# All gathers of a chunk wait for both rounds of the products of the step ahead

## The chip, the cores and the metric

The kernel runs on one core of one Trainium2 chip. A core has five engines that work side by side, each with its own queue of instructions: TensorE (PE; its weight loads are listed apart as PEld), VectorE (DVE), ScalarE (ACT), GpSimd (POOL) and SyncE (SP). They wait for each other through semaphores only. The metric is device time in microseconds (us): 590.68 is the median of 3 runs of the kernel before (590.22 to 592.27).

## The reference

It is a recommendation tower for 2048 samples in float32. Cut to what matters here:

```python
e = stack([tbl_f[ids[:, f]] for f in range(26)])      # 2048 x 26 x 64, rows of 26 tables
x = layer_norm(dense @ Wd.T, gd, bd)                   # 2048 x 128
y = layer_norm(e @ Ws.T, gs, bs)                       # 2048 x 26 x 128
y = layer_norm(einsum('bne,pn->bep', y, Wsi), gsi, bsi)
T = concatenate([x[:, None], swapaxes(y, 1, 2)])       # 2048 x 33 x 128
Z = einsum('bnd,bmd->bnm', T, T)                       # the products: 33 x 33 per sample
z = layer_norm(Z[lower triangle] @ Wl.T, gl, bl)       # first 384 columns are kept
h = relu(relu([z, dense] @ W_top1 + b1) @ W_top2 + b2)
out = h @ W_top3
```

The 53248 table rows of 64 values (2048 x 26) have to be fetched by index. That is the gather.

## The kernel before, in words

The samples are split into 16 units of 128. A unit is worked in 4 chunks; chunk c of unit u has the number k = 4u+c here. Its 1664 rows of the tables lie in `emb[:, u % 3]` as 13 tiles of 128 partitions with two rows side by side. One indirect DMA on GpSimd's queue, L314, fetches 128 rows (one half of a tile), so there are 26 of them in a unit, in four groups for c = 0 to 3: 8, 6, 6 and 6 (`HALVES`, which also splits each group in a first part of 4 gathers and a second of 4, 2, 2 and 2). `emb` has three buffers (`EB`).

The order of work is written out by hand as a pipeline of steps s: each engine runs through the same steps, and in a step it does fixed parts of chunks of different age. On TensorE step s holds, in this order:

- `turn` of chunk s-1 (L382): transposes of the gathered tiles into `bank_t`. It waits for all gathers of its chunk to land (`emb_in`). It raises `turned`.
- `mix` of chunk s-2 (L405): the mixing of the 26 rows into `bank_u`. It raises `mixed`.
- `gram` of chunk s-1 (L391), and `project` of chunk s-2 (L416).
- `products` of chunk s-4 (L430), in two rounds of 16 matmuls: round 0 into `bank_z`, round 1 into `bank_t`, which raise `z_done` by one each (`NR` = 2).
- then, in some steps only, matmuls of the later layers: `top1` (L465), `flat` (L442), `top2`, `dense_x`, `turn_z` and others.

ScalarE copies what comes out of the banks, VectorE scales and sums. The copies of the products go to `zbig`, from which SyncE's queue moves them once per unit.

GpSimd's queue holds nothing but the gathers, in the order of the chunks. Ahead of the gathers of chunk k it waits for `mixed` (the buffer of `emb` is free) and for `turned` of chunk k-2. These two waits stand in L306 and L307. Ahead of the second part of a group it waits in L310 for `z_done` at 2(k-5)+1, which is round 0 of the products of chunk k-5. TensorE does those products in step k-1; the transposes of chunk k stand in step k+1. `after` leaves a wait out while its value is zero or less, so L310 waits from chunk 5 on (at chunk 5 for round 0 of chunk 0).

Only GpSimd's block is changed. `turn`, `products` and the last lines of the diff are enough to follow it.

Of the kernel before, what the change touches and what calls it, by code (L numbers as in the profile page):

```python
# [63 lines left out]
HALVES = ((0, 2), (2, 4)), ((4, 6), (6, 7)), ((7, 9), (9, 10)), ((10, 12), (12, 13))  # L64
# [3 lines left out]
NR = len(ROUNDS)  # L68
# [106 lines left out]
def dlrm(nc, x_in, out):  # L175
    with ExitStack() as ctx:
        def sb(name, shape, dt=F32):
            return ctx.enter_context(nc.sbuf_tensor(name, shape, dt))
# [4 lines left out]
        def sem(name):  # L183
            return ctx.enter_context(nc.semaphore(name))
# [50 lines left out]
        part = sb("part", [P, MAXD])  # L235
# [32 lines left out]
        xcol_ok, z_done, zc_ok, sumcol_ok = sem("xcol_ok"), sem("z_done"), sem("zc_ok"), sem("sumcol_ok")  # L268
# [15 lines left out]
        def after(eng, s, value):  # L284

            if value > 0:
                eng.wait_ge(s, value)
# [12 lines left out]
        @block.gpsimd  # L300
        def _(pool):
            pool.wait_ge(ids_ok, 1)
            for u in range(NU):
                e = u % EB
                for c in range(4):
                    after(pool, mixed, 4 * (u - EB) + min(c + 2, 4))  # L306
                    after(pool, turned, 4 * u + c - 1)  # L307
                    for part, (t0, t1) in enumerate(HALVES[c]):
                        if part == 1:
                            after(pool, z_done, NR * (4 * u + c - 5) + 1)  # L310
                        for t in range(t0, t1):
                            for a in range(2):
                                col = 2 * TILES * u + 2 * t + a
                                pool.indirect_dma_start(  # L314
                                    emb[:, e, t, D * a:D * a + D], None, x_in["tables"],
                                    bass.IndirectOffsetOnAxis(ap=ids[:, col:col + 1], axis=0),
                                ).then_inc(emb_in[e][c], 16)
# [827 lines left out]
```

## Time and profile before

| | |
|---|---|
| median of 3 runs | 590.68 us |
| profiled execution: time | 590.11 us |
| its span, first to last instruction | 588.3 us |
| PE busy | 523.2 us (89%) |
| DVE busy | 431.7 us (73%) |
| ACT busy | 339.3 us (58%) |
| POOL busy | 394.8 us (67%) |
| gathers, L314 | 416, mean 949 ns, idle before them 130.3 us |
| first and last gather start | 4.3 and 524.4 us |
| gather, issue to landing | 2.4 us (median) |
| granted TensorE clock, mean | 0.983 |

How to read it: busy time is time in which an engine works on instructions, not time for which it is needed. "Idle before" is the time that the engine stood still just ahead of a group of instructions, with what ended it; "issue" means that the profile shows nothing that it waited for. For a gather the busy time ends when GpSimd has issued it; the data land later. A start time in the timeline is counted from the first instruction, and start plus duration is the end.

### The profile page before, as it was taken

How to read it: one execution, taken by the hardware profiler on the slowest of the kernel's cores; microseconds unless marked ns; L12 is line 12 of the kernel's file. 1: busy time of each engine (PE TensorE's matmuls, PEld its weight loads, DVE VectorE, ACT ScalarE, POOL GpSimd, SP SyncE). 2: the span in 40 equal slices, each digit the busy share in tenths (PEclk: the TensorE clock that was granted, in tenths of full speed). 3: DMA queues.
4: the chain of work that ended last, by engine and by line, in shares of the span. 5: the costliest groups of instructions: out<-in, count | busy, mean ns of one | idle time of the engine just before them, and what ended most of it. 6: DMA issues, size and time to landing. Idle time of an engine off the chain costs nothing.

```text
span 588.3 us, 11685 instructions
## 1 busy us (share of the span) xinstructions
PE 523.2 (89%) x4327; PEld 382.3 (65%) x4327; DVE 431.7 (73%) x806; ACT 339.3 (58%) x731; POOL 394.8 (67%) x420
## 2 busy tenths in 40 slices
PE   0557889597999999997999999998999999989888
PEld 0435656474778667776677767766777767856657
DVE  3579998689677977697877967796787977787210
ACT  1235666466657765575766765675657765766223
POOL 5777777777777777777777777777777777750000
PEclk9997999899899999999999999999999999999999
DMA  6911121212111121212121221212121211110100
GB/s 214 372 47 26 28 54 27 53 28 52 29 42 38 39 62 28 52 30 71 28 46 33 45 56 35 45 31 69 29 52 27 52 31 43 38 34 17 27 0 1
DMA packets 28152, 29.89 MB, mean 51 GB/s; under 512 B 9784, under 2 KB 20544, under 8 KB 27712
## 3 DMA queue, kind: packets, MB, share of 16 engines
q0 software_dynamic: 13312, 13.66, 12.2%
q1 hardware_dynamic: 14456, 15.29, 8.2%
q8 instruction: 35, 0.57, 0.4%
q10 hardware_dynamic: 328, 0.20, 0.1%
q14 instruction: 21, 0.17, 0.1%
HBM read 23.01 MB, written 0.01 MB: 39 GB/s over the span
## 4 chain that ended last, share of the span: by engine, by line
POOL 46%; PE 26%; issue 19%; DMA 4%; DVE 3%; ACT 1%; ACTq 1%; POOLq 0%; SPq 0%
POOL emb L314 46%; PE bank_h L442 5%; PE bank_u L405 4%; DMA emb<-in_tables,ids 3%; PE bank_m L465 3%; PE bank_y L416 3%; PE bank_g L391 2%; PE bank_z L430 2%; PE bank_t L382 2%; PE bank_t L430 1%; PE bank_m L526 1%; DVE part L910 1%; ACTq L774 1%; PE bank_g L490 1%; PE bank_m L533 0%
## 5 line engine op out<-in xcount | busy, mean ns | idle before, releaser
L314 POOL DMA_INDIRECT emb<-in_tables,ids x416 | 394.6, 949 | 130.3 <-issue 123.1
L662 ACT ACTIVATE sq<-tt 128x512 f32<-128x512 f32 x128 | 131.1, 1133 | 4.6 <-DVE tt L963 3.4
L932 DVE TENSOR_TENSOR prod<-bank_g,emb 128x512 f32<-128x512 f32 (+1 forms) x64 | 37.6, 588 | 89.0 <-PE bank_g L391 88.5
L442 PE MATMUL bank_h<-wz,zr 128*128 128x512 f32 x192 | 93.2, 610 | 3.1 <-ACT zt L727 2.1
L405 PE MATMUL bank_u<-mix_w,emb 128*128 128x192 f32 (+4 forms) x512 | 86.0, 314 | 9.7 <-DVE emb L951 9.7
L405 PEld LDWEIGHTS bank_u<-mix_w,emb 128*128 128x128 f32 x512 | 80.3, 200 | 10.9 <-DVE emb L951 10.9
L963 DVE TENSOR_TENSOR tt<-bank_y,biasc 128x512 f32<-128x512 f32 x128 | 81.9, 681 | 2.5 <-PE bank_y L416 2.5
L644 ACT COPY embt<-bank_t 128x512 f32<-128x512 f32 (+1 forms) x64 | 32.5, 507 | 82.4 <-PE bank_t L382 82.2
L980 DVE TENSOR_TENSOR tt<-tt,bank_z 128x1024 f32<-128x1024 f32 x64 | 78.1, 1220 | 2.2
L970 DVE TENSOR_REDUCE ssum<-sq 128x32 f32<-128x1024 f32 x64 | 77.5, 1211 | 1.1 <-ACT sq L662 1.0
L416 PE MATMUL bank_y<-us,proj 64*128 64x512 f32 x256 | 73.0, 647 | 0.7 <-ACT us L654 0.7
L430 PEld LDWEIGHTS bank_z<-tt 128*64 128x64 f32 x1024 | 35.4, 137 | 48.5 <-issue 47.4
L391 PE MATMUL bank_g<-gram_w,embt 128*128 128x128 f32 x416 | 61.9, 290 | 1.7 <-ACT embt L644 1.7
L382 PE MATMUL bank_t<-eye,emb 128*128 128x128 f32 x208 | 36.3, 290 | 27.5 <-DMA emb<-in_tables,ids 27.5
L654 ACT COPY us<-bank_u 128x512 f32<-128x512 f32 x64 | 37.5, 586 | 40.2 <-PE bank_u L405 40.1
L391 PEld LDWEIGHTS bank_g<-gram_w,embt 128*128 128x128 f32 x416 | 55.2, 202 | 2.7 <-ACT embt L644 2.5
L382 PEld LDWEIGHTS bank_t<-eye,emb 128*128 128x128 f32 x208 | 25.1, 146 | 48.5 <-DMA emb<-in_tables,ids 37.5
L442 PEld LDWEIGHTS bank_h<-wz,zr 128*128 128x128 f32 x192 | 33.8, 190 | 30.7 <-issue 26.8
L649 ACT ACTIVATE std<-var 128x8 f32<-128x8 f32 (+1 forms) x64 | 13.6, 212 | 56.4 <-DVE var L942 54.1
L430 PE MATMUL bank_z<-tt 128*64 128x68 f32 x1024 | 44.5, 229 | 0.0
L430 PE MATMUL bank_t<-tt 128*64 128x68 f32 x1024 | 41.2, 223 | 0.0
L465 PE MATMUL bank_m<-zt,w 128*128 128x256 f32 x168 | 40.8, 379 | 0.0
(121 smaller groups left out, 622.5 us busy)
## 6 DMA issues: line engine op xcount, KB each, us to landing
emb<-in_tables,ids POOLq DMA_INDIRECT x416, 2.4
zs<-zbig SPq DMA_DIRECT2D x62, 40.5 KB
zs<-zbig SPq DMA_DIRECT2D x62, 36.0 KB
dense<-in_dense SPq DMA_DIRECT2D x8, 256.0 KB, 5.1
wfull<-in_wfull SPq DMA_DIRECT2D x1, 2048.0 KB, 10.2
wz<-in_wrows SPq DMA_DIRECT2D x1, 1536.0 KB, 13.2
w<-in_w SPq DMA_DIRECT2D x1, 1280.0 KB, 13.9
zs<-zbig SPq DMA_DIRECT2D x62, 16.5 KB
```

What stands on the lines that cost most here:

```text
L314: pool.indirect_dma_start(emb[:, e, t, D * a:D * a + D], None, x_in["tables"], bass.IndirectOffsetOnAxis(ap=ids[:, col:col + 1], axis=0),) ...
L382: mm = pe.transpose(bank_t[:, P * (t - t0):P * (t - t0) + P], emb[:, e, t, :], eye[:, :])
L391: mm = pe.matmul(bank_g[:, o:o + P], embt[:, k % 2, o:o + P], gram_w[:, :], start=True, stop=True)
L405: mm = pe.matmul(bank_u[:, o:o + PR * cnt], emb[:, e, t, :], mix_w[:, t, :, :].rearrange("p s v -> p (s v)")[:, w0:w0 + PR * cnt], start=( ...
L416: mm = pe.matmul(bank_y[a][:, :], proj[q, :], us[q, h % 2, :], start=True, stop=True)
L430: mm = pe.matmul(o_bank[TILE * q:TILE * q + TILE, o:o + ZC * WIDE], some[:, C0 * WIDE:ZC * WIDE], some, start=True, stop=True)
L442: mm = pe.matmul(bank_h[:, :], zr[:, s, :], wz[:, s, :], start=(s == 0), stop=(s == SLOTS - 1))
L465: mm = pe.matmul(bank_m[:, SUP * (c % 2):SUP * (c % 2) + SUP], w1[:, t, P * c:P * c + P], rhs, start=(t == 3), stop=(t == 2))
L662: A(sq[:, GRP * a:GRP * a + GRP, :].rearrange("p (q w) v -> p q v w", w=WIDE), tt[:, u % 2, q0:q0 + n, C0:ZC, :], ACT.Square).then_inc(sq_ ...
L963: TT(tt[:, u % 2, q0:q0 + n, C0:ZC, :], bank_y[a][:, :].rearrange("p (q w v) -> p q v w", w=WIDE, v=PR), biasc[:, :].unsqueeze(1).unsqueez ...
L970: dve.tensor_reduce(ssum[:, h % 2, :], sq[:, :, :], AX.X, ALU.add).then_inc(ssum_ok, 1)
L980: TT(y, y, srs.rearrange("p (q w) -> p q w", w=WIDE).unsqueeze(2).broadcast_to([P, n, PR, WIDE]), ALU.mult).then_inc(t_ok, 1)
```

## The change

The wait for `z_done` moves from between the two parts of a group of gathers to ahead of the whole group, and its value rises by one, from 2(k-5)+1 to 2(k-4): both rounds of the products of chunk k-5. The two parts are then issued one after the other. No gather is added, removed or reordered.

```diff
--- before.py
+++ after.py
@@ -305,9 +305,8 @@
                 for c in range(4):
                     after(pool, mixed, 4 * (u - EB) + min(c + 2, 4))
                     after(pool, turned, 4 * u + c - 1)
-                    for part, (t0, t1) in enumerate(HALVES[c]):
-                        if part == 1:
-                            after(pool, z_done, NR * (4 * u + c - 5) + 1)
+                    after(pool, z_done, NR * (4 * u + c - 4))
+                    for t0, t1 in HALVES[c]:
                         for t in range(t0, t1):
                             for a in range(2):
                                 col = 2 * TILES * u + 2 * t + a
```

## Rows read from the trace of the kernel before

**Rows 1.** Page, parts 1 and 4: busy us, share, instructions; chain by engine.

```profile
PE 523.2 (89%) x4327; PEld 382.3 (65%) x4327; DVE 431.7 (73%) x806; ACT 339.3 (58%) x731; POOL 394.8 (67%) x420
...
POOL 46%; PE 26%; issue 19%; DMA 4%; DVE 3%; ACT 1%; ACTq 1%; POOLq 0%; SPq 0%
```

**Rows 2.** Gather line L314, 60 to 526 us: durations; idle us, times, by releaser.

```profile
L314 POOL DMA_INDIRECT emb<-in_tables,ids x373: 940/944/957, 60.0 to 524.4; - x187
...
  issue: 110.6, 363
  PE bank_t L382: 3.0, 10
```

**Rows 3.** Transpose line L382, 60 to 528 us: idle us, times, by releaser.

```profile
  DMA emb<-in_tables,ids: 56.0, 35
```

**Rows 4.** Timeline (start us, us, instruction, idle and releaser), chunk 32's products to ScalarE.

```profile
305.98 0.69 PE L430 MATMUL bank_z<-tt 128*64 128x68 f32 x16
...
306.72 0.39 ACT L675 COPY zbig<-bank_z 128x272 f32<-128x272 f32 x1 [0.17 <-PE bank_z L430]
```

**Rows 5.** Timeline, 40 to 62 us: gathers of chunk 5, products of chunk 0.

```profile
48.27 0.94 POOL L314 DMA_INDIRECT emb<-in_tables,ids  x1 [0.30 <-issue]
...
49.52 1.10 POOL L314 DMA_INDIRECT emb<-in_tables,ids  x1 [0.30 <-issue]
49.63 2.46 DVE L921 TENSOR_SCALAR wz<-wz,gq 128x512 f32<-128x512 f32 x6
...
50.92 1.28 POOL L314 DMA_INDIRECT emb<-in_tables,ids  x1 [0.30 <-issue]
...
52.29 0.69 PE L430 MATMUL bank_z<-tt 128*64 128x68 f32 x16
...
52.81 0.64 PE L430 MATMUL bank_t<-tt 128*64 128x68 f32 x16
...
53.76 0.94 POOL L314 DMA_INDIRECT emb<-in_tables,ids  x1 [0.30 <-PE bank_t L430]
```

**Rows 6.** Timeline, 0 to 5 us: POOL's first gather and what released it.

```profile
3.44 0.59 DVE L871 CUSTOM_DVE_ANT_0 ids<-row,ids 128x832 uint16<-128x832 uint16 x1 [1.04 <-DMA row<-in_row]
...
4.32 1.08 POOL L314 DMA_INDIRECT emb<-in_tables,ids  x1 [3.87 <-DVE ids L871]
```

**Rows 7.** Timeline, five stretches: transposes that waited for landing gathers.

```profile
104.94 0.55 PE L382 MATMUL bank_t<-eye,emb 128*128 128x128 f32 x3 [1.09 <-DMA emb<-in_tables,ids]
...
147.36 1.07 PE L382 MATMUL bank_t<-eye,emb 128*128 128x128 f32 x4 [4.16 <-DMA emb<-in_tables,ids]
...
202.32 0.31 PEld L382 LDWEIGHTS bank_t<-eye,emb 128*128 128x128 f32 x3 [0.46 <-DMA emb<-in_tables,ids]
...
408.04 0.66 PE L382 MATMUL bank_t<-eye,emb 128*128 128x128 f32 x4 [2.47 <-DMA emb<-in_tables,ids]
...
462.58 0.55 PE L382 MATMUL bank_t<-eye,emb 128*128 128x128 f32 x3 [0.17 <-DMA emb<-in_tables,ids]
```

**Rows 8.** Timeline, four stretches: first gather of chunks 14, 18, 36, 38, products before.

```profile
121.17 0.94 POOL L314 DMA_INDIRECT emb<-in_tables,ids  x1 [0.30 <-issue]
...
121.61 0.64 PE L430 MATMUL bank_t<-tt 128*64 128x68 f32 x16
...
153.23 0.64 PE L430 MATMUL bank_t<-tt 128*64 128x68 f32 x16
...
153.63 0.94 POOL L314 DMA_INDIRECT emb<-in_tables,ids  x1 [0.30 <-issue]
...
298.10 0.64 PE L430 MATMUL bank_t<-tt 128*64 128x68 f32 x16
...
298.47 0.94 POOL L314 DMA_INDIRECT emb<-in_tables,ids  x1 [0.30 <-issue]
...
315.95 0.94 POOL L314 DMA_INDIRECT emb<-in_tables,ids  x1 [0.30 <-issue]
315.97 0.64 PE L430 MATMUL bank_t<-tt 128*64 128x68 f32 x16
```

## The prediction

> **What bounds the kernel now.** I read the page's busy line first, and it misleads: PE 89% busy, POOL 67% [rows 1]. The chain of waits puts 46% of the span on POOL's gathers and 26% on PE, with 19% "issue" [rows 1]. So the next view is the gather line by itself. From 60 us to the end of its work POOL issues 373 gathers of 944 ns, and before each it is idle for 0.30 us: 110.6 us in 363 gaps named "issue", 3.0 us in 10 named after PE, which is the same 0.30 each [rows 2]. The longest gather in this stretch is 957 ns. So a gather takes 0.94 + 0.30 = 1.25 us of POOL with nothing between, 26 of them (one unit) 32.5 us, and 16 units 520 us; first start 4.3, last 524.4. The 33% of POOL that is not busy is no room: it is that fixed gap. POOL never waits for anybody after the start, so **its queue is the clock of the kernel up to 525 us**, and the 63 us behind the last gather are the tail.
>
> PE follows it: in this stretch it (with its weight loads) waited 35 times, 56.0 us in all (its two queues counted together), for a landing gather before the transposes of a chunk [rows 3]. PE alone would be a little faster than POOL on the average and is slower in some steps. It falls behind by up to some 3 us and catches up.
>
> **The change part by part.** I number chunks k = 4u+c from 0. Chunk k has 8 gathers if c = 0, else 6; chunk 14 starts with the 93rd gather, chunk 18 with the 119th, 36 with the 235th, 38 with the 249th, 52 with the 339th, 54 with the 353rd. The products of a chunk are one group of 16 matmuls into bank_z (round 0) and one into bank_t (round 1), so those of chunk k-5 are the (k-4)th such pair; they run in step k-1, in which POOL starts the gathers of chunk k.
>
> *Removed:* the wait ahead of the last 2 (c = 0: 4) gathers of a chunk for round 0 of chunk k-5. The 0.30 us gap stands with or without it, and it never held POOL, so it gives 0.
>
> *Added:* the same semaphore one count higher (round 1), ahead of the first gather of every chunk from 5 on. Its instruction itself costs 0, because it stands where two others already do and the gap there is the same 0.30. What counts is that everything behind it on POOL is gathers alone, so a stall shifts all later ones, and PE waits for these. POOL has no other DMA or move behind it, and SP's queue is untouched.
>
> So for each chunk: slack = start of its first gather minus end of round 1 of chunk k-5, and the new wait stalls by release time minus slack where that is positive. *The release time* (last matmul's end to a POOL start) is nowhere in the trace as such. From below: ScalarE starts 0.05 us after the end of a round [rows 4]. From above: the fifth gather of chunk 5 already waits for round 0 of chunk 0, which ended at 52.29 + 0.69 = 52.98; it starts at 53.76, so 0.78 is the most it can be [rows 5]. Nearest is POOL's own one real wait: VectorE's add ends at 3.44 + 0.59 = 4.03 and the first gather starts at 4.32, 0.29 us [rows 6]. I take 0.3.
>
> *Start-up, chunk 5.* Its first gather starts at 48.27; round 1 of chunk 0 ends at 52.81 + 0.64 = 53.45 [rows 5], late because VectorE still prepares weights. Stall 5.18 + 0.3 = 5.5. Two of its gathers took 1.10 and 1.28 us there, beside six scalings of wz on VectorE (49.63 to 52.09) [rows 5]; after the stall they lie behind these and take 0.94, which gives back 0.16 + 0.34 = 0.5. Net 5.0. The Trainium skill, "SBUF — State Buffer", section "SBUF: two separate sides", says that a VectorE operation in a two-port mode locks POOL out of the shared port, so that descriptors aren't written; the trace agrees in sign (1.28 against 0.94). By it alone one would look for gains in where gathers fall against VectorE, but in the steady part the longest gather is 0.957, so there is nothing to win there.
>
> Is this absorbed? PE has a few us of room over these landings, but at chunk 11 its transposes wait again for the gathers, at 104.94 with 1.09 us idle [rows 7]. From there PE is late by all that POOL is late: **+5.0**.
>
> *Steady part.* While POOL and PE are shifted alike, the slacks of before hold. When POOL alone is held (PE did not wait for gathers there, thus isn't late), the shift of POOL grows and that of PE doesn't; PE's products then come early relative to POOL, so the next slack is larger by that difference, until a turn that waits for a landing makes both equal again. Such turns: 147.36 (chunk 16, 4.16 us idle), 202.32 (chunk 23), 408.04 (chunk 48, 2.47 us), 462.58 (chunk 55) [rows 7]. Walking along all chunks, the slack is 0.3 to 4 us in most and below 0.3 in these [rows 8]:
> - chunk 14: gather 121.17, round ended 121.61 + 0.64 = 122.25, slack -1.08: stall 1.4. Chunk 15's slack is then covered. PE equal again at 16.
> - chunk 18: 153.63 - (153.23 + 0.64) = -0.24: stall 0.5. Equal again at 23.
> - chunk 36: 298.47 - (298.10 + 0.64) = -0.27: 0.6; chunk 38: 315.95 - (315.97 + 0.64) = -0.66: needs 1.0 and has 0.6, so 0.4 more. Chunk 39 is covered. Equal again at 48.
> - chunks 52 and 54 repeat 36 and 38 sixteen chunks later (two such pairs in all): 0.6 + 0.4. Equal again at 55.
> - chunks 22, 30, 46 and 62 come within 0.05 of the limit: 0.2 together.
>
> Sum 1.4 + 0.5 + 1.0 + 1.0 + 0.2 = 4.1. The tail is behind a last gather that PE waits for, and nothing in it depends on this semaphore, so it hides nothing. In all 5.0 + 4.1 = **+9.1 us**. The profiled execution took 590.11 (its span 588.3), which gives 599.2; the median shown is 590.68, 0.57 higher, so I predict **599.8**.
>
> Ends of the range: with a release of 0.05 the same walk gives 4.8 + 3.0 = 7.8. With 0.78 the thin slacks count too (chunks 28, 34, 44, 50, 60 and again 30, 46, 62, by 0.1 to 0.4 each) and it gives 5.5 + 7.5 = 13.
>
> **The rivals.** *A, start-up alone:* the steady stalls vanish, because PE, no longer fed ahead of time, orders its steps so that it isn't behind at chunks 36 and 38. For it: their slacks are within 1 us of the limit. Against it: PE is behind there by its own heavier steps (products of the last layers), not by gathers; it didn't wait for one between chunks 32 and 39. Then +5.0, 595.7.
>
> *B, slow release:* the first gather behind a real wait needs as long as the upper bound allows. For it: POOL has to start from rest, and three waits stand in a row. Against it: the 0.29 at 4.32. Then +13, 603.7; each further 0.1 us costs some 0.8.
>
> *C, not slower:* POOL catches up after a stall, since its 0.30 us gaps are issue time that could be prepared while it waits. For it: 123 us of gaps, and 33% idle. It decides if the gap behind a stall shrinks to 0.28 (0.02 less in each of 416 gives 8 us). Then the stalls cost nothing, 590.7, and with the stretched gathers of the start gone as well (0.5 in chunk 5) 590.2. Against it: no gap in the page is shorter, not even behind the 4 us that POOL waited at the start.
>
> *D, the wait doesn't bite:* the count is reached already. It would give 590.7, but chunk 5 starts 5.2 us before the matmul that sets it [rows 5], so this can't be for that one.
>
> **How the numbers follow.** Forecast (7.8 to 11): 0.60. A: 0.14. B: 0.20. C and D: 0.06, of which 0.02 faster. A measurement of this kernel can tell 0.3% (1.8 us) from no change. So faster 0.02, same 0.04, slower 0.94. The range reaches to A's lower side and over B: 595.8 to 605.
>
> **What would show it.** On POOL, a gap of about 5.5 us ahead of the gather that started at 48.27, released by PE bank_t, and then not 404 equal gaps but some ten longer ones of 0.4 to 1.7 us, the first at about 126 us, then one each some 16 chunks later in pairs; gathers still 944 ns; last gather at 533.5; PE's waits for landings in about the same places; tail still 63 us. Wrong on the release if the gap at chunk 5 is 6 us; wrong on the ledger if there are gaps in every unit; wrong altogether if the gaps of 0.30 shrink behind a stall, or if the last gather starts before 527.

## The result and the profile after

| | before | changed |
|---|---|---|
| median, beside each other | 591.42 us (590.22 to 592.27, 4 runs) | 609.36 us (608.53 to 612.52, 4 runs) |
| ratio | | 1.0327, 95% interval 1.0305 to 1.0349 |
| profiled execution / its span | 590.11 / 588.3 us | 608.53 / 606.7 us |
| last gather starts | 524.4 us | 543.0 us |
| granted TensorE clock, mean | 0.983 | 0.969 |

A second comparison on another chip gave 611.38 against 591.46, ratio 1.0347 (1.0317 to 1.0377). The forecast was +9.1, the result is +17.9 in the medians.

The page of the changed kernel, parts 1 and 4 (busy us, share of the span, instructions; then the chain of waits by engine and by line); they answer to [rows 1]:

```profile
PE 530.2 (87%) x4327; PEld 386.2 (64%) x4327; DVE 431.8 (71%) x806; ACT 341.2 (56%) x731; POOL 394.5 (65%) x420
...
POOL 39%; PE 32%; issue 17%; DMA 7%; DVE 2%; ACT 1%; ACTq 1%; POOLq 0%; SPq 0%
```

POOL's busy time is the same, and so is DVE's. PE has the same 4327 matmuls and is busy 7 us longer. The chain passed from POOL to PE and the landing of gathers: the two now wait for each other. The gather line of the changed kernel over the whole run (durations; then idle time of POOL before them, times, by releaser), against [rows 2]:

```profile
L313 POOL DMA_INDIRECT emb<-in_tables,ids x416: 938/944/1274, 4.4 to 543.0; - x139
its engine sat idle before it (us, times) until:
  issue: 123.2, 396
  PE bank_t L429: 22.0, 19
```

Before, everything that was not "issue" was the same 0.30 us. Now there are 22.0 us for PE, in bank_t's round. Sixteen gaps are over 0.4 us. They stand at chunk 5 (5.32), 10 (1.97), 14 (2.00), 18 (1.92), 28 (0.51), 30 (0.69), 34 (2.32), 36 (1.01), 38 (0.69), 42 (0.62), 44 (1.03), 46 (0.70), 50 (2.35), 52 (1.05), 54 (0.69) and 62 (0.70). Less 0.30 each, that is 5.0 us at chunk 5 and **13.75 us** in the other fifteen; 18.6 us is what the last gather starts later. So the whole loss is in these sixteen gaps, and the tail behind the last gather is as long as before (63.7 against 63.9 us).

The first gap, in the timeline of the changed kernel (start us, us, instruction, idle before and releaser), against [rows 5]:

```profile
52.11 0.64 PE L429 MATMUL bank_t<-tt 128*64 128x68 f32 x16
53.54 0.94 POOL L313 DMA_INDIRECT emb<-in_tables,ids  x1 [5.32 <-PE bank_t L429]
```

The round ends at 52.75 and the gather starts 0.79 us behind it. All sixteen gaps end 0.78 to 0.81 us behind the last matmul of the round. The prediction took 0.3. The chain that ended last, followed back through this gap, shows what lies between (start us, us, what):

```profile
52.28 0.50 PE bank_t L429 x16
52.78 0.02 issue
52.80 0.02 POOLq L287
52.82 0.72 issue
53.54 0.94 POOL emb L313
```

L287 is the `wait_ge` inside `after`, as an instruction of its own in GpSimd's queue. It ends 0.72 us ahead of the gather, here and in the other fifteen gaps.

The gap at chunk 34 is one of the long ones. Same columns:

```profile
288.60 0.65 PE L381 MATMUL bank_t<-eye,emb 128*128 128x128 f32 x4 [2.52 <-DMA emb<-in_tables,ids]
289.09 1.66 PE L404 MATMUL bank_u<-mix_w,emb 128*128 128x64 f32 x8
290.54 1.92 PE L390 MATMUL bank_g<-gram_w,embt 128*128 128x128 f32 x8
292.39 1.57 PE L415 MATMUL bank_y<-us,proj 64*128 64x512 f32 x4
...
294.41 0.64 PE L429 MATMUL bank_t<-tt 128*64 128x68 f32 x16
...
295.87 0.94 POOL L313 DMA_INDIRECT emb<-in_tables,ids  x1 [2.32 <-PE bank_t L429]
```

From the transposes of chunk 32 (288.60) to the end of the products of chunk 29 (295.05) it takes 6.45 us. In the kernel before the same stretch took 4.85 (278.18 to 283.03). The eight matmuls of L390 last 1.92 us here and 1.05 in the same step before. The stretches table shows why (stretch, its length, busy us and count of PE, PEld, DVE, ACT, POOL, granted PE clock, DMA share, GB/s), first changed, then before:

```profile
290.00:292.00 2.00, 2.00 (x10) 2.00 (x10) 0.00 (x0) 1.21 (x3) 1.59 (x2) 0.50 0.15 30
```

```profile
280.00:282.00 2.00, 2.00 (x16) 1.12 (x17) 1.05 (x2) 1.98 (x5) 1.63 (x2) 1.00 0.18 33
```

**The granted clock was 0.50 there (1.2 of 2.4 GHz)** and 1.00 in the same step before. Ahead of it TensorE had stood idle for 2.52 us, waiting for chunk 32's gathers. Behind chunk 8, where it waited longer, the step is slower still:

```profile
87.26 1.12 PE L381 MATMUL bank_t<-eye,emb 128*128 128x128 f32 x4 [5.49 <-DMA emb<-in_tables,ids]
...
88.17 2.45 PE L404 MATMUL bank_u<-mix_w,emb 128*128 128x64 f32 x8
...
95.14 0.94 POOL L313 DMA_INDIRECT emb<-in_tables,ids  x1 [1.97 <-PE bank_t L429]
```

The Trainium skill, "TensorE: Matmul & The Clock Gate", section "HAM oscillation — how this bites in real kernels", says that an array whose wait for DMA is long enough falls back from 2.4 to 1.2 GHz. These rows agree in the two levels, 1.00 and 0.50.

The length of the idle stretch alone doesn't tell whether the clock falls. The same transposes stood behind 2.36 us of idle time before the change, at full clock, and those of chunk 48 behind 2.47 us before (full clock) and 2.45 us after (half). Of the five places at half clock up to the last gather, chunks 12 and 16 were at half before the change too; chunks 8, 32 and 48 are new. Only at chunk 8 is the idle stretch clearly longer than before (5.49 against 1.75 us).

### The profile page after: what moved, and what is told of

It reads as the page before. It is cut to its first block, busy times and chain, and to the rows that moved or that the text cites. A ratio compares the mean times of both kernels' runs of the same rounds, so it can differ in the third digit from the quotient of the medians.

```text
span 606.7 us, 11692 instructions
## 1 busy us (share of the span) xinstructions
PE 530.2 (87%) x4327; PEld 386.2 (64%) x4327; DVE 431.8 (71%) x806; ACT 341.2 (56%) x731; POOL 394.5 (65%) x420
## 4 chain that ended last, share of the span: by engine, by line
POOL 39%; PE 32%; issue 17%; DMA 7%; DVE 2%; ACT 1%; ACTq 1%; POOLq 0%; SPq 0%
POOL emb L313 39%; DMA emb<-in_tables,ids 6%; PE bank_u L404 6%; PE bank_h L441 5%; PE bank_y L415 4%; PE bank_g L390 4%; PE bank_m L464 3%; PE bank_z L429 3%; PE bank_t L381 2%; PE bank_t L429 2%; PE bank_m L525 1%; PE bank_m L532 1%; DVE part L909 1%; ACTq L773 1%; PE bank_g L489 1%
## 5 line engine op out<-in xcount | busy, mean ns | idle before, releaser
L404 PE MATMUL bank_u<-mix_w,emb 128*128 128x192 f32 (+4 forms) x512 | 88.4, 319 | 8.2 <-DVE emb L950 8.2
L404 PEld LDWEIGHTS bank_u<-mix_w,emb 128*128 128x128 f32 x512 | 82.7, 204 | 8.9 <-DVE emb L950 8.9
L381 PE MATMUL bank_t<-eye,emb 128*128 128x128 f32 x208 | 37.8, 299 | 43.0 <-DMA emb<-in_tables,ids 42.8
L390 PE MATMUL bank_g<-gram_w,embt 128*128 128x128 f32 x416 | 63.4, 295 | 1.0 <-ACT embt L643 1.0
L390 PEld LDWEIGHTS bank_g<-gram_w,embt 128*128 128x128 f32 x416 | 57.4, 209 | 1.7 <-ACT embt L643 1.7
```

The lines of the kernel that those rows point to most:

```text
L381: mm = pe.transpose(bank_t[:, P * (t - t0):P * (t - t0) + P], emb[:, e, t, :], eye[:, :])
L390: mm = pe.matmul(bank_g[:, o:o + P], embt[:, k % 2, o:o + P], gram_w[:, :], start=True, stop=True)
L404: mm = pe.matmul(bank_u[:, o:o + PR * cnt], emb[:, e, t, :], mix_w[:, t, :, :].rearrange("p s v -> p (s v)")[:, w0:w0 + PR * cnt], start=( ...
```

## The experiments

Each was compared with the kernel before on its own chip; times are medians. A sum of gaps is over POOL's gaps of more than 0.4 us, less 0.30 each; a single gap is given whole. "Steady" means all but chunk 5's. Comments inside the diffs are mine.

**e1: the new wait at chunk 5 only.**

```diff
+                    if 4 * u + c == 5:
+                        after(pool, z_done, NR * (4 * u + c - 4))
                     for part, (t0, t1) in enumerate(HALVES[c]):
```

> The kernel before, with the new wait (both rounds) ahead of the gathers of chunk 5 alone; all other chunks wait as before. Theory: the start-up stall is a shift of GpSimd's queue that nothing absorbs: one gap of 5.3 us ahead of chunk 5's first gather, less 0.5 us of stretched gathers, so 591.4 + 4.5 to 5 = about 596. Where GpSimd has no wait later on, a slower TensorE step costs nothing. Rival: TensorE, held longer before chunk 8, is late for good (lower granted clock and all), and the time is 600 or more.

Measured: 595.89 against 592.05, ratio 1.0074 (1.0048 to 1.0100): +3.8. In its timeline there is one gap and no other:

```profile
53.65 0.94 POOL L316 DMA_INDIRECT emb<-in_tables,ids  x1 [5.27 <-PE bank_t L432]
```

The last gather starts at 529.3, 4.9 later than before. And the clock falls here too, for example behind chunk 32:

```profile
284.00:286.00 2.00, 2.00 (x9) 2.00 (x9) 0.00 (x0) 0.58 (x1) 1.39 (x3) 0.50 0.10 17
```

What follows: the start-up stall costs about what the prediction said. The clock is at half in five places before the last gather, as in the changed kernel, and nothing is lost by it: up to the last gather a step at half clock costs nothing as long as POOL doesn't wait for its products.

**e2: no start-up stall, the new wait from chunk 10 on.**

```diff
+                    if 4 * u + c >= 10:
+                        after(pool, z_done, NR * (4 * u + c - 4))
...
-                        if part == 1:
+                        if part == 1 and 4 * u + c < 10:
```

> The kernel before up to chunk 9, the changed one from chunk 10 on, so no start-up stall. Theory (release of 0.8 us, and the granted clock): the thin slacks alone give +7.7 us by the walk with 0.8 us; steps at half clock behind chunks that TensorE waits longer for add 2 to 5: 599 to 604, with stalls of about 2 us at chunks 14, 18, 34 or 50. Rival (the start-up stall is what sets off the rest): at most +4, 595, with stalls under 0.6 us.

Measured: 606.55 against 592.05, ratio 1.0248 (1.0223 to 1.0272): +14.5, with gaps of 2.3 us at chunks 34, 42 and 50. That is above the 599 to 604 that I expected. So the steady stalls stand on their own; the start-up stall doesn't set them off. 3.8 and 14.5 add up to 18.3, the whole change within the noise. In the trace of e2 the steady gaps sum to 13.0 us. The tail behind the last gather is 65.4 us there, against 63.9 before: the clock was at half once more, at 569 us.

**e3 and e12: keep TensorE busy.** The changed kernel, with matmuls without use ahead of the wait for the gathers, so that the clock stays up. e3 fills the places where the changed kernel's clock fell; e12 adds the two that fell next.

```diff
-                pe.wait_ge(emb_in[e][k], 16 * 2 * (t1 - t0) * (u // EB + 1))
                 after(pe, embt_ok, 4 * u + k)
                 after(pe, zc_ok, NR * (4 * u + k - 3))
+                for _ in range(FILL.get(4 * u + k, 0)):   # {8: 10, 12: 9, 16: 9, 32: 4, 48: 4}, e12 also 40: 4, 56: 4
+                    pe.matmul(bank_t[:, 0:384], eye[:, :], ..., start=True, stop=True)
+                pe.wait_ge(emb_in[e][k], 16 * 2 * (t1 - t0) * (u // EB + 1))
```

> The changed kernel, with idle TensorE given filler matmuls (128x384, into bank_t, overwritten by the transposes) just ahead of the wait for the gathers of chunks 8, 12 and 16 (10, 9, 9 of them) and 32, 48 (4 each); nothing else changed. Theory: TensorE's granted clock falls to half behind those idle stretches, this makes the next products 1.5 to 2 us late, and GpSimd waits for them (gaps of 2 us at chunks 10, 14, 18, 34, 50). With the clock kept, these gaps shrink to 0.3 to 0.9 us and the time falls by 5 to 7 us, to 602.5 to 604.5; granted clock 0.98. Rival: the clock is only a bystander, the steps are long by their work: time within 1 us of 609.4, or longer by the fillers' own time, gaps still 2 us.

Measured: 607.19 against 592.05, ratio 1.0245 (1.021 to 1.028). The gaps at chunks 14, 18, 34 and 50 went from 2.00, 1.92, 2.32 and 2.35 us to 0.73, 0.81, 0.77 and 0.78, as the clock theory says. But the time, which I expected at 602.5 to 604.5, fell less. Three things in the trace stand against it: the clock fell somewhere new, with a gap of 2.42 at chunk 42; chunk 5's gap was 7.27 here, since round 1 of chunk 0 ended 1.8 us later; and the clock was at half at 572 us, with a tail of 65.6 us in place of 63.7.

> As the kernel with fillers ahead of the gathers of chunks 8, 12, 16, 32 and 48, with 4 more ahead of those of 40 and 56, where the granted clock fell next (a gap of 2.4 us at chunk 42). Theory: no step at half clock is left before 560 us; the gap at chunk 42 falls from 2.4 to about 0.8, and the steady gaps (all but chunk 5's) add to 9 to 10 us beyond 0.30, against 15.7 in the changed kernel and 11.6 with five places filled; time 603 to 606, by how long chunk 5's gap is (5.3 or 7.3). Rival: another chunk falls to half clock instead and nothing is won.

Measured: 605.72 against 590.42, ratio 1.0249 (1.0226 to 1.0271). The granted clock is 1.00 from 54 us on, 0.992 in the mean. The place shown above for chunk 34, now:

```profile
285.42 2.75 PE L381 MATMUL bank_t<-mix_w,eye 128*128 128x384 f32 x8
...
288.00 0.60 PE L385 MATMUL bank_t<-eye,emb 128*128 128x128 f32 x4
...
292.15 0.64 PE L433 MATMUL bank_t<-tt 128*64 128x68 f32 x16
...
293.61 0.94 POOL L314 DMA_INDIRECT emb<-in_tables,ids  x1 [0.72 <-issue]
```

288.00 to 292.79 is 4.79 us, as before the change, and the gap is 0.72 for 2.32. The seventeen steady gaps sum to 9.1 us against 13.75. So **the half clock is worth 4.6 us**, net of what the fillers themselves delay: behind chunk 8's last gather the transposes start 4.15 us after its start in place of 2.53. What is left, 9.1, stands 1.6 above the 7.5 that the prediction's own walk gave for a release of 0.78; chunks 10, 42 and 58, which the walk didn't have, hold 1.8 of it. The time itself doesn't show the whole of it, because chunk 5's gap was 7.28 here.

**e4: no wait for products at all.**

```diff
-                    after(pool, z_done, NR * (4 * u + c - 4))
```

> GpSimd waits for no products at all; only the two waits for the buffer and for the transposes stay. Theory: the wait of the kernel before never held GpSimd, so 591.4 within 1 us, and gaps of 0.30 us throughout. Rival: keeping gathers away from the products helped TensorE or the landings, and the time is longer by over 2 us.

Measured: 591.41 against 592.05, ratio 0.9991 (0.9979 to 1.0003), and no gap of POOL over 0.31 us behind the start. The old wait held nobody.

**e5 and e6: position and count apart.** The change does two things; each alone:

```diff
-                    after(pool, z_done, NR * (4 * u + c - 4))
+                    after(pool, z_done, NR * (4 * u + c - 5) + 1)      # e5: new place, old count
```

> The position of the change without its count: the wait stands ahead of the first gather of a chunk, for round 0 alone. Round 0 ends 0.47 us ahead of round 1, so each slack is larger by that: the walk with an effective release of 0.33 gives +9, the half clock adds 3 to 5: 603 to 605, ten or so gaps. Rival (the second round is what makes the wait bite): within 2 us of 592.

Measured: 607.66 against 590.42, ratio 1.0295 (1.0253 to 1.0336), 3 us above what I expected. Gaps end 0.31 to 0.34 us behind round 1, that is 0.8 behind round 0; those at chunks 10, 14 and 18 are 1.90, 1.99 and 1.96, nearly as long as with both rounds; why they aren't shorter by 0.47 us isn't shown. The steady gaps sum to 9.7 us against 13.75, with four places at half clock against five; chunk 5's gap was 6.07, and the tail 65.5 with the clock at half at 572 us.

```diff
                         if part == 1:
-                            after(pool, z_done, NR * (4 * u + c - 5) + 1)
+                            after(pool, z_done, NR * (4 * u + c - 4))   # e6: old place, new count
```

> The count of the change without its position: the wait for both rounds stays between the two parts. The slack there is 3.75 us (three gathers more... four gathers of 1.25 us less the round) above that of the first gather, over 4 us from chunk 9 on, so only chunk 5 can wait, by 0.3 to 0.8 us: 591.5 to 593, no gap over 0.4 elsewhere. Rival: the second round counts, and it is over 595.

Measured: 590.64 against 590.42, ratio 1.0002 (0.9987 to 1.0017). One gap, at the fifth gather of chunk 5. The rows of e6:

```profile
53.05 0.64 PE L430 MATMUL bank_t<-tt 128*64 128x68 f32 x16
53.98 0.94 POOL L314 DMA_INDIRECT emb<-in_tables,ids  x1 [0.63 <-PE bank_t L430]
```

The position does the harm. The count alone does none at the old place; at the new place the second round adds to the steady gaps (e5: 9.7 us without it, 13.75 with it). And here the gather starts 0.29 us behind the matmul, not 0.8. The chain through this gap has no L287 in it:

```profile
53.22 0.50 PE bank_t L430 x16
53.72 0.26 issue
53.98 0.94 POOL emb L314
```

Here z_done is the only wait at its place; ahead of a chunk it stands behind others.

**e9: another releaser.** z_done is replaced by zc_ok, ScalarE's copies of the two rounds.

```diff
-                    after(pool, z_done, NR * (4 * u + c - 4))
+                    after(pool, zc_ok, NR * (4 * u + c - 4))
```

> The changed kernel, but GpSimd waits for ScalarE's copies of both rounds (zc_ok) in place of the matmuls (z_done). This measures the release by another engine. Theory: the 0.8 us from the last matmul to the gather is GpSimd's own restart, the same for every releaser, so the gather starts 0.75 to 0.8 us behind the end of the copy, 1.2 us or more behind the last matmul, and the time is over 613. Rival: 0.5 us of the 0.8 belongs to the matmul (its real end is later than its record) and ScalarE releases in 0.3; then the gather starts 0.75 us behind the matmul as before, and the time stays near 609.

Measured, one run: 613.68. The rows at chunk 10:

```profile
94.31 0.64 PE L429 MATMUL bank_t<-tt 128*64 128x68 f32 x16
...
95.00 0.39 ACT L674 COPY zbig<-bank_t 128x272 f32<-128x272 f32 x1
96.15 0.94 POOL L313 DMA_INDIRECT emb<-in_tables,ids  x1 [1.99 <-ACT zbig L674]
```

0.76 us behind the copy, 1.20 behind the matmul. All twenty gaps of this trace end 0.76 to 0.80 us behind a copy. The 0.8 us is POOL's own and not the matmul's.

**e10, e13, e7, e11, again as e14 to e17, and e18.** They were to tell whether a row of waits makes the release 0.8. The kernel before itself took 774, 763 and 761 us in these three comparisons, on three chips, against 590 to 592 in all others (two of these three chips among them), so their times can't be set beside the rest. I call 590 to 592 us for the kernel before the ordinary condition. e10, e14 and e18 are one kernel, with one wait ahead of a chunk:

```diff
-                    after(pool, mixed, 4 * (u - EB) + min(c + 2, 4))
-                    after(pool, turned, 4 * u + c - 1)
+                    if 4 * u + c < 5:
+                        after(pool, turned, 4 * u + c - 1)
                     after(pool, z_done, NR * (4 * u + c - 4))
```

e13 and e15 add e12's fillers to it; e7 and e17 put z_done first of three waits; e11 and e16 are the kernel before with fillers at chunks 12 and 16.

> The changed kernel, where from chunk 5 on z_done is the only wait ahead of a chunk's first gather (it implies the other two: TensorE has done those transposes and that mixing before these products). Theory: the release of 0.79 to 0.81 us is the price of a wait that stands in a row with others; alone it was 0.28 (the one wait in the kernel with both rounds at the old place). Then gathers start 0.3 us behind the last matmul, the walk gives +9, the half clock adds its 3 to 5: 602 to 605. Rival: the place ahead of a chunk, or the length of the pause, makes it 0.8: release unchanged, time 608 to 610.

> Both at once: one wait from chunk 5 on, and fillers at chunks 8, 12, 16, 32, 40, 48, 56. Theory: release 0.3 and no half clock leave what the prediction's walk counted, +9 (steady gaps of 4 to 5 us beyond 0.30, at about chunks 14, 18, 36, 38, 52, 54), and +1 to 2 where chunk 5's gap falls long: 599 to 602. Rival: there is a third cause, and the time stays over 604.

> The changed kernel with the order of the three waits turned round: z_done first, then mixed, then turned. Theory: what costs is that two waits stand beside it at all; each instruction behind it adds, so the release is 0.8 or more and the time 608 to 612. Rival: only the last of the three sits with the gather, and the release falls to 0.3.

> The kernel before with fillers at the two chunks (12: 9, 16: 8) behind which its own granted clock falls to half. Theory: there GpSimd does not wait for products, so slow TensorE steps cost nothing: 591 to 592.5, clock 0.985 or more. Rival: the half clock costs the kernel before as well, and it gains 2 us or more.

> The changed kernel, where from chunk 5 on z_done is the only wait ahead of a chunk's first gather (it implies the other two), again, on a chip where the kernel before takes 590 to 592 us. Theory: a release of 0.28 where z_done waits alone, against 0.79 to 0.81 in a row of waits; then the walk gives +9 and the half clock 3 to 5: 602 to 605. Rival: the place ahead of a chunk, or the pause, makes it 0.8, time 608 to 610.

> Both at once: one wait from chunk 5 on, and fillers at chunks 8, 12, 16, 32, 40, 48, 56. Theory: release 0.3 and no half clock leave what the prediction's walk counted, +9 (steady gaps of 4 to 5 us beyond 0.30), and 1 to 2 more where chunk 5's gap falls long: 599 to 602. Rival: there is a third cause, and the time stays over 604.

> The kernel before with fillers at the two chunks (12: 9, 16: 8) behind which its own granted clock falls to half. Theory: there GpSimd does not wait for products, so slow TensorE steps cost nothing: within 1 us of the kernel before, clock 0.985 or more. Rival: the half clock costs the kernel before as well, and it gains 2 us or more.

> The changed kernel with the order of the three waits turned round: z_done first, then mixed, then turned. Theory: the release depends on where in the row the wait stands that comes last; with z_done first it is no longer than 0.3 us, since the others are met already, and the time is that of the kernel with one wait, 602 to 605. Rival: each further wait behind it adds, the release stays 0.8 or grows, and the time is 608 to 612.

> The changed kernel, where from chunk 5 on z_done is the only wait ahead of a chunk's first gather. On a chip where the kernel before takes 590 to 592 us: theory (a row of waits makes the release long) 0.28 from the last matmul to the gather, and 602 to 605; rival (the place ahead of a chunk, or the pause, makes it 0.8) 0.8 and 608 to 610.

Measured, ratio to the kernel before beside them: e10 752.52, 0.9733 (0.9677 to 0.9789); e14 739.73, 0.9755 (0.9677 to 0.9832); e18 740.31, 0.975 (0.9651 to 0.985); e13 772.26, 0.999 (0.9957 to 1.0022); e15 764.76, 1.0029 (0.999 to 1.0068); e7 758.42, one run; e17 740.49, 0.9759 (0.9688 to 0.9831); e11 792.48, 1.0244 (1.0169 to 1.0318); e16 778.37, 1.0248 (1.0179 to 1.0317). The fillers didn't come out as expected there: e13 and e15 are 20 and 25 us slower than e10 and e14, e11 and e16 are 18 and 15 us slower than the kernel before, where a gain or no change was expected.

In these comparisons POOL stands still where it waits for nothing. In e7, e10, e13, e14, e15, e17 and e18 the gap ahead of a chunk whose wait was long met is 1.7 to 1.9 us, and 2.9 to 3.8 behind a group of eight gathers. The rows of e18 at chunk 12:

```profile
123.30 0.64 PE L429 MATMUL bank_t<-tt 128*64 128x68 f32 x16
127.04 0.94 POOL L313 DMA_INDIRECT emb<-in_tables,ids  x1 [1.77 <-remote]
```

In e11 and e16 it isn't each place: ahead of 25 and 20 of the chunks from 6 on the gap is 0.30 us.

**What these traces do settle is the release.** Where the wait binds in e7, e10, e14, e17 and e18, the gather starts 0.27 to 0.36 us behind the matmul, 0.27 to 0.30 in most cases, with one wait and with z_done first of three alike. In e16, where `turned` binds, both releases stand side by side at the same place, ahead of a chunk. At chunk 8 `turned` is the only wait (`mixed` begins at chunk 12); at chunk 22 it stands behind `mixed`, which is met. The rows of e16:

```profile
82.30 0.85 PE L386 MATMUL bank_t<-eye,emb 128*128 128x128 f32 x3
...
83.42 0.94 POOL L315 DMA_INDIRECT emb<-in_tables,ids  x1 [2.90 <-PE bank_t L386]
...
244.15 0.60 PE L386 MATMUL bank_t<-eye,emb 128*128 128x128 f32 x4
...
245.52 0.94 POOL L315 DMA_INDIRECT emb<-in_tables,ids  x1 [2.40 <-PE bank_t L386]
```

That is 0.27 us with one wait and 0.77 with two, with pauses of like length. The same holds at chunks 3, 6 and 8 (0.27) and at all 23 chunks from 14 on where `turned` binds (0.77 to 0.78). The count of L287 on POOL's queue says which wait it is. The changed kernel has 59, one for each chunk with more than one wait; e6 has 52, for the chunks with `mixed` and `turned`; e18, with one wait at each place, has none; e17 has 59 again. So the wait that is written first goes with the gather itself and releases it in 0.28 us, and those behind it form an instruction of their own, 0.72 us ahead of the gather. The change wrote z_done last. What fills the 0.72 us isn't shown, and what z_done written first would save in the ordinary condition was not measured.

**e20: the changed kernel once more.**

> The changed kernel itself, unaltered, once more. If the kernel before takes 590 to 592 us here, it takes 608 to 611 again. If it takes 755 to 775, as in the last three comparisons, where each place with a wait on GpSimd's queue cost about 1.8 us whether met or not: the kernel before has two such places in a chunk and the changed one has one, so theory says that the changed kernel is the faster there by 2 to 3% (735 to 750 us), like the two variants with one such place; rival: the stalls by late products come on top and it is as slow as before or slower. The release, with z_done written last: 0.28 if the order or number of waits does not matter there, 0.8 if it does.

Measured: 611.38 against 591.46, ratio 1.0347 (1.0317 to 1.0377), release 0.78 to 0.81 again, chunk 5's gap 6.47 us, the tail 65.4 us with the clock at half at 575 us, gaps at the same chunks but with the clock falling ahead of chunk 42 in place of 34 (2.16 us against 0.62 in the first trace; at 34 0.55 against 2.32). Where it falls varies from run to run; it fell five times before the last gather in both traces. This comparison fell in the ordinary condition, so whether the changed kernel is the faster one in the other condition was not tried.

## Why the prediction was wrong

- *The bound, the direction and the mechanism*: right. POOL's queue was the clock of the kernel, the gathers still take 944 ns, and every us that POOL waits is lost (18.6 us of gaps, 18.4 of span).
- *Removed wait worth 0, instruction worth 0*: right (e4, e6).
- *One reading*: the 33% of POOL that is not busy is not all the fixed gap. Of 193 us, 130 are gaps and 63 are the tail. Nothing else hung on it.
- *Start-up, +5.0*: right in size, +3.8 by e1 (4.9 in its last gather), but two errors cancel in it. In the changed kernel's trace round 1 of chunk 0 ended at 52.75 in place of 53.45, 0.70 us earlier, and the release was 0.49 us longer than taken. So the sign "wrong on the release if the gap at chunk 5 is 6 us" couldn't show the slow release: the gap was 5.32. The 0.5 us given back came as forecast (7.48 us from chunk 5 to chunk 6 against 7.98). I hadn't seen that this term varies: the gap was 5.3 to 7.3 from run to run and kernel to kernel.
- *The release, 0.3*: **the first step that failed.** It was 0.78 to 0.81 in every binding wait ahead of a chunk, the upper bound that I had given, not POOL's start at 4.32 that I took as nearest. That row has one wait ahead of it, which goes with the gather; z_done is the last of two or three at its place and an instruction of its own, 0.72 us ahead of the gather. By the prediction's own ledger this is +3.9 (13 for 9.1).
- *"While POOL and PE are shifted alike, the slacks of before hold"*: **the second step that failed.** It takes the length of PE's steps as given. The kernel before had its clock at half in two stretches after the start, and I read them neither in the stretches nor in the transposes of [rows 7], where 1.07 us for four stands beside 0.66. In the changed kernel the clock is at half in five places up to the last gather. Those steps are 1.6 to 2.3 us longer from the transposes to the products than the same step at full clock (4.85 us), and POOL now waits for just those steps. That is 4.6 us (e12 against the changed kernel). The waiting is what's new, and not so much the clock: e1 has five such places too and loses nothing by them. Why the clock falls at chunks 32 and 48, behind idle stretches as long as before, stays open.
- *The ledger itself*: the chunks were right (14, 18, 36, 38, 52, 54, and with 0.78 also 28, 30, 34, 44, 46, 50, 62, and 60 with 0.37 us just under my limit; 10 and 42 were missing), the sum at 0.78 short by 1.6.
- *Sum*: 9.1 + 3.9 + 4.6 = 17.6, for 17.9 measured. That it closes so well is partly luck, as the 1.6 us and the varying start-up are in neither the sum nor the noise of one trace.
- *Rival A* (start-up alone) fell: the steady part alone is +14.5 (e2). *B* (slow release) had the release right, and its reason, waits in a row, was the cause; its 603.7 is short by 5.7 us, 4.6 of them the clock. *C* (gaps shrink behind a stall) fell: they are 0.30 all through.

## What to carry to other kernels

When a queue that issues back to back gets a new wait, each slack has to be taken with the longest release that the trace allows, since thin slacks in every period multiply it. Where several waits stand at one place, write the one that binds first: on GpSimd's queue it released in 0.28 us as the first (e17), and in 0.8 as the last (the changed kernel, e16). And a wait couples two engines both ways: ask what the other engine's idle time does to its clock. A slow step off the critical path is free until somebody waits for it (e1 against the changed kernel). Between two places for the same wait, take the one where the slack is 5 us, not 1 (e6 against the changed kernel).

## What the runs showed of the hardware

- GpSimd starts a gather 0.27 to 0.29 us behind the event where it waits for one semaphore (e6, chunk 8 of e16, and at its first gather) or where the binding wait is the first of three (e17). It starts 0.76 to 0.81 us behind it where the binding wait stands behind one or two others that are met (all sixteen gaps of the changed kernel and those of e1, e2, e3, e12 and e20, released by PE; those of e9, released by ACT; 23 chunks of e16). The later waits are an instruction of their own, which ends 0.72 us ahead of the gather.
- TensorE's granted clock fell to 0.50 at the transposes with idle stretches of 2.0 to 5.5 us ahead of them. All stretches of 3.58 to 5.49 us had it at half in or behind them; of those of 2.0 to 2.5 us some had it (2.16 us, chunk 48 of e1) and some not (2.47 us ahead of 408.04 in the kernel before).
- A stretch at half clock in the tail, at 569 to 575 us, goes with a tail of 65.4 to 65.6 us (e2, e3, e5, e20) in place of 63.7 to 63.9 (the kernel before, the changed one, e1, e12).
- In three comparisons on three chips POOL stood still for 1.7 us or more at places whose wait was long met, at most places but not all (e11, e16), and the kernel before took 752 to 782 us in place of 591. There the variants with one place with waits per chunk and no fillers (e10, e14, e17, e18) had ratios of 0.973 to 0.976 to the kernel before, which has two, with intervals up to 0.985. What brings this about is open: two of the chips had run at 590 to 592 before.
